# Cross-attention stage of a decoder layer: query and key parts kept in DRAM in blocks of four heads with a gap, each part stored by its own transfer

## The chip, the cores and the metric

One Trainium2 chip, one core of it. The metric is the device time of one execution of the whole kernel in microseconds (us). Before the change it is 2364.4 us, the median of 3 runs (2364.01 to 2364.47).

## The reference, cut to what matters

The kernel computes one decoder layer with the norm behind each part, on 32 sequences of 256 tokens and 256 features: self-attention, cross-attention to 120 context tokens, and a mixture of experts. The change lies in the cross-attention:

```python
q = query @ qw.T + qb            # query: the 256 tokens of a sequence, 16 heads of 16
k = key @ kw.T + kb              # key: its 120 context tokens
v = value @ vw.T + vb
q1, q2 = (q[..., :sd], q[..., sd:])      # each head is cut in two halves of sd = 8
k1, k2 = (k[..., :sd], k[..., sd:])
a1 = softmax(einsum('bhtd,bhsd->bhts', q1, k1) * SCALING)
a2 = softmax(einsum('bhtd,bhsd->bhts', q2, k2) * SCALING)
attn_output = einsum('bhts,bhsd->bhtd', a1 - lam * a2, v)
```

## The kernel before, in words

Four stages run one after the other: `self_attention`, `cross_attention`, `experts`, `finish`. A barrier of all engines stands between the attention stages. The cross stage works through 32 batches, one sequence each, as a software pipeline of steps: in step t a batch t is loaded (X), t-1 is projected (A, lag 1), t-2 has its stacks loaded (B, lag 2), t-3 has the maxima of its scores taken (M, lag 3), t-4 has its scores, exponentials and products with the values computed (S, lag 4), t-5 is put together (O), t-6 is normed and routed to experts (R), and t-7 is scattered into the slot table (Q). Buffers have three slots. Every engine runs its own list of a step in a fixed, hand-written order and waits on semaphores; no planner is at work. The middle of the run is a hardware loop over three steps at a time.

To keep the precision of float32 in bf16 matmuls, the projected queries and keys are split into three bf16 parts. ScalarE makes part 0 (line 1341), GpSimd the rest (1618), ScalarE part 1 (1373), GpSimd part 2 (1623). The tile `parts` has 128 partitions, one for each pair of a dimension d (8) and a head h (16), with d the slower one, and 2 x 256 query and 2 x 120 key columns for each part (the factor 2 is the two halves e of a head). A matmul needs d on the partitions and the heads along the row, so the parts are turned around through DRAM. Lines 1011 to 1015 store them with four transfers for a batch (for each e one for q, one for k, all three parts in one). Lines 984 to 990 load them back: a row of DRAM that holds all 16 heads of one (part, d) becomes one partition of `q_stack` (16 x 256 elements of 2 bytes, 8192 bytes) or `k_stack` (16 x 120, 3840 bytes). `STACK_LOADS` has seven loads for each e (four for q with 8, 8, 16 and 16 rows, three for k with 24, 16 and 8), because parts repeat in the stack: six pairs of parts by 8 dimensions make 48 rows. So 14 loads a batch bring 96 rows of 8192 and 96 rows of 3840 bytes.

All these transfers are issued by SyncE (SP). Its list of a step is: x and context of X (970, 971), residual of S (976), wait for the parts of B in DRAM (980) and for the scores that used its slot (983), the 14 stack loads of B (989), the stores of R and Q (993, 996), wait for the transposed maxima of M and three small loads of them into the last rows of `q_stack` (999 to 1002), wait for part 2 of A (1007), and the stores of the parts of A (1011 to 1015).

TensorE (PE) first uses the stacks of batch B in `max_scores(B, 0)` (line 1053), which waits for all 14 loads (line 1045) and stands behind `scores(S, 5)` in the step. Behind it in the same step comes the transpose of the maxima of M (1218), which ScalarE copies (1381) and SP waits for at line 999 (DMA of line 1001). VectorE reduces each set of max scores (1423). ScalarE's line 1340 waits until the parts of the batch before are in DRAM, before it overwrites them. GpSimd (POOL) scatters batch Q into the slot table with 12 indirect DMAs (1592): seven at the start of its step, three behind line 1618, two behind line 1623.

```python
q_dram = nc.dram_tensor("cross_q_parts", [3, E, NP, P, T], BF16, kind="Internal").ap()
sp.dma_start(q_dram[A.slot][e].rearrange("t p n -> p t n"), parts[:, :, e * T:(e + 1) * T])
q_src = q_dram[B.slot][e].rearrange("t (d h) n -> (t d) (h n)", h=NH)
sp.dma_start(stack[e * HALF + row:e * HALF + row + m, B.slot, 0:NH * n], src[src_row:src_row + m, :])
```

## Time and profile before

| what | us |
|---|---|
| median of 3 runs | 2364.4 |
| the profiled execution, its own time | 2375.9 |
| span of the profile, first to last instruction | 2374.1 |
| busy in the span: PE | 1805.2 (76%) |
| busy: VectorE (DVE) | 1297.7 (55%) |
| busy: GpSimd (POOL) | 1230.5 (52%) |
| busy: ScalarE (ACT) | 1085.8 (46%) |
| q1, the DMA queue of SP: share of the 16 DMA engines' time | 45.8% |

A share of busy time is a mean over four stages with different limits. The cross stage lies between about 807 and 1935 us of the span. "Idle before" of an instruction is the time its engine stood still just before it, and the name behind it is what the profile holds to have ended that: "issue" where it shows nothing, "remote" where the semaphore was raised at a moment at which the profile has no instruction ending. SPq are the DMA issues of SP; their duration is the time of the issue, not of the transfer.

### The profile page before, as it was taken

What the parts mean: (1) busy time and instruction counts of PE and PEld (TensorE: products, weight loads), DVE (VectorE), ACT (ScalarE), POOL (GpSimd) and SP (SyncE); (2) the same over time, 40 slices, a digit from 0 to 9 for tenths busy, and PEclk for the clock granted to TensorE, in tenths of its full rate; (3) what the DMA queues carried; (4) which work ended last, traced back from release to release, by engine and by line L of the source; (5) the groups of instructions that cost most, each with busy time, mean ns of one, the idle gap of its engine ahead of it and who ended that gap; (6) DMA issues with size and microseconds to landing.
All of it is one profiled execution on the core that took longest, in us unless ns stands there. A gap on an engine that the chain in (4) does not pass through costs nothing. (4 is left out here: it accounts for less than half of the span.)

```text
span 2374.1 us, 46091 instructions
## 1 busy us (share of the span) xinstructions
PE 1805.2 (76%) x14688; PEld 1268.9 (53%) x14688; DVE 1297.7 (55%) x3032; ACT 1085.8 (46%) x1670; POOL 1230.5 (52%) x1287
## 2 busy tenths in 40 slices
PE   1499999999998458777778788777887619999900
PEld 1366666666666335545545455454553308888800
DVE  2457667776677247665556655566565412222258
ACT  0356666666666236555555555555553302222200
POOL 1557667766773112555555555555555444554523
PEclk9799999999999769888788777887876759999955
DMA  5656766676665266444444344543342024555545
GB/s 184 138 137 147 175 152 155 157 173 153 158 152 123 69 110 129 87 88 72 89 93 90 75 71 90 93 93 79 73 76 52 17 57 109 131 126 124 113 110 180
DMA packets 288970, 267.14 MB, mean 113 GB/s; under 512 B 78962, under 2 KB 273364, under 8 KB 278640
## 3 DMA queue, kind: packets, MB, share of 16 engines
q1 hardware_dynamic: 257648, 244.57, 45.8%
q0 software_dynamic: 22528, 13.03, 3.7%
q10 hardware_dynamic: 8704, 8.39, 1.1%
q8 instruction: 50, 0.82, 0.2%
q14 instruction: 40, 0.33, 0.1%
HBM read 170.57 MB, written 94.30 MB: 112 GB/s over the span
## 5 line engine op out<-in xcount | busy, mean ns | idle before, releaser
L1423 DVE TENSOR_REDUCE cross_nmax<-cross_p_mx 128x8 f32<-128x960 f32 x256 | 295.2, 1153 | 351.6 <-DMA self_q_stack<-self_nmaxT 220.6
L1592 POOL DMA_INDIRECT slot_table<-cross_tok_i,cross_slot_i x384 | 379.6, 989 | 126.9 <-issue 107.0
L598 DVE TENSOR_REDUCE self_nmax<-self_p_mx 128x2 f32<-128x512 f32 x512 | 329.0, 687 | 209.8 <-PE self_p_mx L340 209.5
L1279 ACT ACTIVATE cross_probs<-cross_p_sc 120x1024 f32<-120x1024 f32 x256 | 261.5, 1021 | 113.4 <-PE cross_p_sc L1037 81.4
L510 ACT ACTIVATE self_probs<-self_p_sc 128x1024 f32<-128x1024 f32 x256 | 261.3, 1021 | 94.7 <-PE self_p_sc L328 92.4
L1069 PE MATMUL cross_p_pv<-cross_probs,cross_v_aug 120*32 120x256 f32 x2048 | 199.2, 462 | 14.4 <-ACT cross_o_raw L1287 5.8
L340 PE MATMUL self_p_mx<-self_k_stack,self_q_stack 96*128 96x256 bf16 x1024 | 160.4, 277 | 64.4 <-DMA self_k_stack<-self_k_parts 60.6
L1053 PE MATMUL cross_p_mx<-cross_k_stack,cross_q_stack 48*128 48x120 bf16 x2048 | 118.5, 247 | 119.2 <-DVE cross_nmax L1423 86.8
L1037 PE MATMUL cross_p_sc<-cross_q_stack,cross_k_stack 51*128 51x256 bf16 x1024 | 118.4, 317 | 85.6 <-issue 47.4
L1053 PEld LDWEIGHTS cross_p_mx<-cross_k_stack,cross_q_stack 48*128 48x128 bf16 x2048 | 83.8, 111 | 162.0 <-DVE cross_nmax L1423 115.0
L328 PE MATMUL self_p_sc<-self_q_stack,self_k_stack 99*128 99x256 bf16 x1024 | 156.8, 276 | 13.6 <-ACT self_probs L510 12.8
L1939 POOL DMA_INDIRECT expert_sums<-ffn_ye,ffn_idx_add x64 | 92.3, 1442 | 121.6 <-DMA expert_sums<-ffn_ye,ffn_idx_add 65.5
L1618 POOL TENSOR_TENSOR cross_qk_rest<-cross_qk,cross_parts 128x752 f32<-128x752 f32 x32 | 51.6, 1613 | 188.5 <-ACT cross_parts L1341 188.5
L340 PEld LDWEIGHTS self_p_mx<-self_k_stack,self_q_stack 96*128 96x128 bf16 x1024 | 95.8, 98 | 92.0 <-DMA self_k_stack<-self_k_parts 46.1
L355 PE MATMUL self_p_pv<-self_probs,self_v_aug 128*32 128x256 f32 x2048 | 140.5, 393 | 1.4 <-ACT self_probs L510 1.4
L1879 DVE COPY ffn_xgT<-ffn_p 128x384 f32<-128x384 f32 x32 | 17.8, 558 | 224.4 <-PE ffn_p L1809 224.4
L699 POOL TENSOR_TENSOR self_even_cos<-self_qkb,self_cos_t 128x512 f32<-128x512 f32 x32 | 40.9, 1280 | 187.6 <-ACT self_qkb L526 187.6
L328 PEld LDWEIGHTS self_p_sc<-self_q_stack,self_k_stack 99*128 99x128 bf16 x1024 | 86.6, 98 | 93.3 <-ACT self_probs L510 49.8
L1857 ACT ACTIVATE ffn_hT<-ffn_ph 128x512 f32<-128x512 f32 x64 | 38.2, 597 | 210.1 <-PE ffn_ph L1827 193.4
L1827 PE MATMUL ffn_ph<-ffn_xT,ffn_sw 128*128 128x256 f32 x512 | 117.7, 383 | 0.0
L1287 ACT ACTIVATE cross_o_raw<-cross_p_pv 128x512 f32<-128x512 f32 x128 | 76.3, 596 | 88.7 <-PE cross_p_pv L1069 49.6
L1800 PE MATMUL ffn_p<-ffn_sw,ffn_hT 128*128 128x256 f32 x512 | 115.9, 379 | 0.0
(180 smaller groups left out, 3852.5 us busy)
## 6 DMA issues: line engine op xcount, KB each, us to landing
self_q_stack<-self_q_parts SPq DMA_DIRECT2D x64, 256.0 KB, 5.8
cross_q_stack<-cross_q_parts SPq DMA_DIRECT2D x128, 128.0 KB
ffn_w<-in_ffn_w SPq DMA_DIRECT2D x64, 256.0 KB
self_q_parts<-self_parts SPq DMA_DIRECT2D x32, 384.0 KB, 2.8
self_k_parts<-self_parts SPq DMA_DIRECT2D x32, 384.0 KB, 3.8
self_k_stack<-self_k_parts SPq DMA_DIRECT2D x32, 384.0 KB, 8.0
cross_q_parts<-cross_parts SPq DMA_DIRECT2D x64, 192.0 KB
expert_sums<-zero_rows SPq DMA_DIRECT2D x8, 1024.0 KB, 10.2
```

Source lines behind the costliest of these rows:

```text
L328: mm = pe.matmul(p_sc[:, w, kc * T:(kc + 1) * T], k_stack[0:RM, S.slot, k_at:k_at + P], q_stack[0:RM, S.slot, u * T:(u + 1) * T], start=Tr ...
L340: mm = pe.matmul(p_mx[:, m % 2, c * T:(c + 1) * T], q_stack[0:RK, M.slot, q_at:q_at + P], k_stack[0:RK, M.slot, m * T:(m + 1) * T], start= ...
L355: mm = pe.matmul(p_pv[j * SLOT:(j + 1) * SLOT, (p % 2) * T:(p % 2 + 1) * T], v_aug[:, S.slot, kc, u, :], probs[:, (u // 2) % 4, (2 * (u % ...
L510: act.activation(probs[:, g % 4, :], p_sc[:, :, :].rearrange("p b n -> p (b n)"), ACT.Exp, scale=SCALE).then_inc(s_exp, 1)
L598: dve.tensor_reduce(nmax[:, M.slot, :, m], p_mx[:, m % 2, :].rearrange("p (c k) -> p c k", c=TC), AX_X, ALU.max, negate=True).then_inc(s_r ...
L1037: mm = pe.matmul(p_sc[:, e, hh * T:(hh + 1) * T], k_stack[r:r + RM, S.slot, h * KEYS:h * KEYS + P], q_stack[r:r + RM, S.slot, h * T:(h + 1 ...
L1053: mm = pe.matmul(p_mx[:, e, (2 * hh + c) * KEYS:(2 * hh + c + 1) * KEYS], q_stack[r:r + RK, M.slot, q_at:q_at + P], k_stack[r:r + RK, M.sl ...
L1069: mm = pe.matmul(p_pv[j * SLOT:(j + 1) * SLOT, (g % 2) * T:(g % 2 + 1) * T], v_aug[0:KEYS, S.slot, e, 2 * g + hh, :], probs[0:KEYS, g % 4, ...
L1279: act.activation(probs[0:KEYS, g % 4, :], p_sc[0:KEYS, :, :].rearrange("p b n -> p (b n)"), ACT.Exp, scale=SCALE).then_inc(s_exp, 1)
L1423: dve.tensor_reduce(nmax[:, M.slot, :, :, 2 * m:2 * m + 2].rearrange("p c e h -> p e h c"), p_mx[:, :, 0:4 * KEYS].rearrange("p e (x k) -> ...
L1592: pool.indirect_dma_start(out=route[:, :], out_offset=bass.IndirectOffsetOnAxis(ap=slot_i[:, Q.slot, tc, k:k + 1], axis=0), in_=tok_i[:, Q ...
L1827: mm = pe.matmul(p_h[:, k // 2, (k % 2) * T:(k % 2 + 1) * T], sw1[:, f, k * P:(k + 1) * P], xT[:, f, :], start=(f == 0), stop=(f == FC - 1))
```

## The change

The DRAM tensors of the parts get another shape. A part is no longer 128 rows of n columns (n = 256 for q, 120 for k), but 32 blocks. A block holds four heads of one dimension, 4 x n elements, and 32 unused elements (64 bytes) behind them. A stack row is then four pieces of 2048 bytes (q) or 960 bytes (k) that don't touch in DRAM, in place of one run of 8192 or 3840 bytes. There are still 14 loads a batch. Each of the three parts is stored by a transfer of its own: 12 stores a batch in place of 4, with the same bytes. The counts that wait for the stores grow by the factor 3 (NP).

```diff
+    PIECE, GAP = 4, 32
-    q_dram = nc.dram_tensor("cross_q_parts", [3, E, NP, P, T], BF16, kind="Internal").ap()
-    k_dram = nc.dram_tensor("cross_k_parts", [3, E, NP, P, KEYS], BF16, kind="Internal").ap()
+    q_dram = nc.dram_tensor("cross_q_parts", [3, E, NP, P // PIECE, PIECE * T + GAP], BF16, kind="Internal").ap()
+    k_dram = nc.dram_tensor("cross_k_parts", [3, E, NP, P // PIECE, PIECE * KEYS + GAP], BF16, kind="Internal").ap()
...
-                    n_pw = held(sp, 64 * (B.turn + 1))
+                    n_pw = held(sp, 64 * NP * (B.turn + 1))
...
-                        q_src = q_dram[B.slot][e].rearrange("t (d h) n -> (t d) (h n)", h=NH)
-                        k_src = k_dram[B.slot][e].rearrange("t (d h) n -> (t d) (h n)", h=NH)
+                        q_src = q_dram[B.slot][e].rearrange("t (d b) x -> (t d) b x", b=NH // PIECE)
+                        k_src = k_dram[B.slot][e].rearrange("t (d b) x -> (t d) b x", b=NH // PIECE)
                         for is_q, row, src_row, m in STACK_LOADS:
                             stack, src, n = (q_stack, q_src, T) if is_q else (k_stack, k_src, KEYS)
-                            sp.dma_start(stack[e * HALF + row:e * HALF + row + m, B.slot, 0:NH * n],
-                                         src[src_row:src_row + m, :]).then_inc(s_st[B.slot], 16)
+                            sp.dma_start(stack[e * HALF + row:e * HALF + row + m, B.slot, 0:NH * n]
+                                         .rearrange("p (b x) -> p b x", x=PIECE * n),
+                                         src[src_row:src_row + m, :, 0:PIECE * n]).then_inc(s_st[B.slot], 16)
...
                     for e in range(E):
-                        sp.dma_start(q_dram[A.slot][e].rearrange("t p n -> p t n"),
-                                     parts[:, :, e * T:(e + 1) * T]).then_inc(s_pw[A.slot], 16)
-                        sp.dma_start(k_dram[A.slot][e].rearrange("t p n -> p t n"),
-                                     parts[:, :, QW + e * KEYS:QW + (e + 1) * KEYS]).then_inc(s_pw[A.slot], 16)
+                        for t in range(NP):
+                            sp.dma_start(q_dram[A.slot][e][t][:, 0:PIECE * T].rearrange("r (i n) -> r i n", n=T),
+                                         parts[:, t, e * T:(e + 1) * T]).then_inc(s_pw[A.slot], 16)
+                            sp.dma_start(k_dram[A.slot][e][t][:, 0:PIECE * KEYS].rearrange("r (i n) -> r i n", n=KEYS),
+                                         parts[:, t, QW + e * KEYS:QW + (e + 1) * KEYS]).then_inc(s_pw[A.slot], 16)
...
-                        act.wait_ge(s_pw[last.slot], 64 * (last.turn + 1))
+                        act.wait_ge(s_pw[last.slot], 64 * NP * (last.turn + 1))
```

## Rows read from the trace of the kernel before

**Rows 1.** Waits, 900 to 1790 us: us in total, times, longest.

```profile
DVE cross_nmax L1423 <- DMA self_q_stack<-self_nmaxT: 201.2, 28, 8.1
...
PEld cross_p_mx L1053 <- DMA cross_k_stack<-cross_k_parts: 3.0, 1, 3.0
```

**Rows 2.** Timeline, one steady step: start us, us, engine, line [idle before].

```profile
1298.99 1.10 POOL L1592 DMA_INDIRECT slot_table<-cross_tok_i,cross_slot_i  x1 [0.84 <-POOL cross_tok_i L1608]
...
1306.80 0.97 POOL L1592 DMA_INDIRECT slot_table<-cross_tok_i,cross_slot_i  x1 [0.30 <-issue]
...
1309.16 1.16 DVE L1423 TENSOR_REDUCE cross_nmax<-cross_p_mx 128x8 f32<-128x960 f32 x1 [7.98 <-DMA self_q_stack<-self_nmaxT]
```

**Rows 3.** Timeline, a step of the drain, behind the last stack loads.

```profile
1837.82 0.97 POOL L1592 DMA_INDIRECT slot_table<-cross_tok_i,cross_slot_i  x1 [0.30 <-issue]
...
1840.95 0.28 ACT L1349 ACTIVATE cross_gate_e<-cross_p_b 128x128 f32<-128x128 f32 x1 [7.61 <-remote]
```

**Rows 4.** Windows: stretch, its length, busy us of PE, PEld, DVE, ACT, POOL, PEclk, DMA share, GB/s.

```profile
1308.00:1310.00 2.00, 0.39 (x4) 0.11 (x4) 0.84 (x1) 1.44 (x3) 0.00 (x0) 0.94 0.01 0
1301.00:1309.00 8.00, 4.01 (x38) 2.59 (x37) 0.18 (x1) 2.23 (x4) 5.25 (x6) 1.00 0.58 109
1825.00:1841.00 16.00, 11.59 (x80) 5.71 (x76) 3.13 (x4) 3.24 (x5) 10.72 (x11) 0.61 0.02 1
```

**Rows 5.** Timeline of SP and PE, the same steady step.

```profile
1300.30 1.14 SPq L989 DMA_DIRECT2D cross_k_stack<-cross_k_parts  x3
...
1319.75 0.49 PE L1053 MATMUL cross_p_mx<-cross_k_stack,cross_q_stack 48*128 48x120 bf16 x8
...
1322.21 1.65 SPq L1001 DMA_DIRECT2D cross_q_stack<-cross_nmaxT  x3
...
1355.55 1.64 SPq L1001 DMA_DIRECT2D cross_q_stack<-cross_nmaxT  x3
```

**Rows 6.** Waits of the DMA queue of SP, 900 to 1790 us.

```profile
SPq L1001 <- ACT cross_nmaxT L1381: 507.2, 28, 20.1
```

**Rows 7.** Waits, 826 to 950 us.

```profile
PE cross_p_mx L1053 <- DMA cross_k_stack<-cross_k_parts: 20.0, 3, 14.9
```

**Rows 8.** Timeline of PE, 826 to 947 us: max scores of a newly loaded batch.

```profile
848.61 0.58 PE L1053 MATMUL cross_p_mx<-cross_k_stack,cross_q_stack 48*128 48x120 bf16 x8 [14.86 <-DMA cross_k_stack<-cross_k_parts]
...
887.65 0.38 PE L1053 MATMUL cross_p_mx<-cross_k_stack,cross_q_stack 48*128 48x120 bf16 x8 [2.38 <-DMA cross_k_stack<-cross_k_parts]
...
931.22 0.38 PE L1053 MATMUL cross_p_mx<-cross_k_stack,cross_q_stack 48*128 48x120 bf16 x8
```

**Rows 9.** Timeline of SP and PE, one whole turn of the early steps.

```profile
889.74 1.60 SPq L1001 DMA_DIRECT2D cross_q_stack<-cross_nmaxT  x3
891.45 0.38 SPq L1012 DMA_DIRECT2D cross_q_parts<-cross_parts  x1
...
892.98 0.52 SPq L1014 DMA_DIRECT2D cross_k_parts<-cross_parts  x1
...
894.65 0.47 SPq L976 DMA_DIRECT2D cross_x_res<-x_with_bias  x1
896.92 1.69 SPq L989 DMA_DIRECT2D cross_q_stack<-cross_q_parts  x4
...
909.00 0.38 PE L1053 MATMUL cross_p_mx<-cross_k_stack,cross_q_stack 48*128 48x120 bf16 x8 [2.72 <-DMA cross_k_stack<-cross_k_parts]
...
911.22 1.60 SPq L1001 DMA_DIRECT2D cross_q_stack<-cross_nmaxT  x3
```

**Rows 10.** Windows behind the loads of 917.7 to 924.6 us, columns as in group 4.

```profile
930.00:931.00 1.00, 1.00 (x9) 0.70 (x8) 0.90 (x4) 0.68 (x3) 0.00 (x0) 1.00 0.15 53
```

**Rows 11.** DMA issues of the whole run: KB each, median us to landing.

```profile
self_q_stack<-self_nmaxT SPq DMA_DIRECT2D x96, 8.0 KB, 1.9
```

**Rows 12.** Windows: 8192-byte rows at the start of the run, then stack loads alone.

```profile
20.00:23.00 3.00, 0.00 (x0) 0.00 (x0) 0.00 (x0) 0.00 (x0) 0.00 (x0) 1.00 1.03 429
852.00:862.00 10.00, 8.16 (x51) 6.22 (x52) 4.94 (x5) 1.21 (x3) 0.00 (x0) 0.50 0.80 99
```

## The prediction

> **What bounds the kernel now.** The change touches only how the parts reach the stacks, so the question is where anything waits for them. I read the waits of the cross stage first. Between 900 and 1790 us, where the pipeline is full, VectorE's reduction stands idle for 201.2 us in 28 waits, 7.2 us each, and the name behind it is a DMA; TensorE waits for the stack loads once, for 3.0 us [rows 1]. The first row is tempting: it falls into the time of the stack loads. The DMA named is one of the self stage, long over, so the name is no evidence. Next I read the timeline of one step. POOL begins seven scatters at 1298.99 and ends them at 1307.77 (1306.80 + 0.97); VectorE's idle time of 7.98 us ends 1.4 us later, at 1309.16 [rows 2]. In the drain, where no stack is loaded any more, the same thing happens behind twelve scatters: the last ends at 1838.79, and ScalarE's idle time of 7.61 us ends at 1840.95, put down to "remote" [rows 3]. The DMA share is 0.58 in the first stretch and 0.02 in the second [rows 4]. So the stall goes with the scatters of GpSimd and not with the stack loads. It sets the steady step of 33.3 us (1322.21 to 1355.55) [rows 5].
>
> The stack loads of that step are issued by 1301.4, the DMA engines are empty from 1308 on (share 0.01), and TensorE first needs them at 1319.75 [rows 4, 5]. That is about 11.7 us of slack. SP itself waits 18.1 us a step (507.2 us in 28 waits) for the transposed maxima [rows 6].
>
> The early steps are different. Before the scatters begin, a turn takes 21.5 us (889.74 to 911.22) [rows 9], and three waits of TensorE, 20.0 us together, are for the stack loads [rows 7]: 14.86 at the first batch, 2.38 at the third, 2.72 at the fourth [rows 8, 9]. There the loop maxima, stores, loads, max scores, maxima is closed through SP's list, and what SP does longer makes the turn longer.
>
> **Eight more stores.** Four stores take 1.53 us for three spacings (891.45 to 892.98), 0.51 us each [rows 9]. Twelve take 8 x 0.51 = 4.1 us more. Queued behind them on SP are x, context, residual and the stack loads. Against that stands the wait for the parts to land. Now the loads start at 896.92, 3.9 us behind the last store's issue, though SP has issued x, context and residual by 895.1 [rows 9]: the four stores (564 KB) are still under way. Spread over 6 us, all but the last are done, and the last holds 30 KB. A transfer of 8 KB lands 1.9 us after its issue [rows 11]; I take 2.4 us. That gives back 1.5 us, and at most 1.8, since the three issues behind the stores still have to be made; at least nothing. So the loads start 4.1 - 1.5 = **2.6 us** later (2.3 to 4.1). The data of the stores is the same, and its runs stay 512 and 240 bytes.
>
> **Pieces of 2048 and 960 bytes.** 14 loads as before, so no more issues; a third dimension may lengthen an issue from 0.4 towards the 0.51 of the stores, at most 14 x 0.1 = 1.4 us, most of it beside the transfers. What the pieces do to the transfers the trace doesn't show; bounds: while stack loads run alone, 12.8 engines are busy (0.80 x 16) and move 99 GB/s, 7.7 GB/s each. Stores of 8192-byte rows from 128 partitions moved 429 GB/s on 16 engines, 26 each [rows 12]. So a row of 8192 bytes is not slow by its length; the engines of a stack load, which has 8 to 24 rows on neighbouring partitions, get in each other's way. The pieces go to the same partitions in the same order. If they cured it, the burst from 896.92 to 909.00, 12.1 us, could shrink to its issue, 14 x 0.4 = 5.6, and one landing, 1.9: 7.5 us, a gain of 4.6 [rows 9, 11]. If the fourfold number of pieces costs, I bound it with 2 us. I take **0.5 us** more, near the old value, since the bytes and partitions stay.
>
> The Trainium skill (SBUF — State Buffer, section "Door 1: The DMA port swizzle") says that the bandwidth of a DMA goes by how many of 16 ports its partitions reach; by it the burst would not change, and the gain of 4.6 falls away. Against the change speaks DMA: Bandwidth & Descriptors, section "How a descriptor splits into AXI transactions": a piece that starts off a 256-byte boundary costs an extra transaction. Blocks of 2112 bytes mostly start off one; my estimate from its beats is up to 12% of the burst, 1.4 us a turn, or 5 us in the sum.
>
> **What of it reaches the end.** A turn that is bound by the loads grows by 2.6 + 0.5 = 3.1 us.
> - First, third and fourth batch: 3 x 3.1 = 9.3.
> - Second batch: no wait in the view now [rows 7]; its loads queue behind the first batch's and move with them. 0 to 3.1, I take 0.4.
> - Fifth batch: TensorE starts on it at 931.22 without a wait, and by 930 to 931 the DMA share is down to 0.15 [rows 8, 10]. Some 1.2 us of cover, so 3.1 - 1.2 = 1.9.
> - The other 27: slack 11.7 against 3.1, cover left. Nothing. If that cover were gone, each turn would pay the excess.
> - Gap and counts: nothing. ScalarE's wait for the stores (line 1340) stands in the next step, behind three exponentials; the turn of 21.5 us or more covers stores that end 4.1 us later.
>
> Sum: 9.3 + 0.4 + 1.9 = 11.6 us. A turn lost early isn't won back, because the later steps are bound by something else and just start later. The profiled execution took 2375.9 us for its span of 2374.1; the median without a profile is 2364.4, 0.5% less. I add the 11.6 to the median: **2376.0 us**. About 0.2%, 4.7 us, is what a measurement of this kernel can tell from no change.
>
> **Rivals.**
> - *A, the pieces free the DMA engines.* For it: 7.7 GB/s an engine against 26 [rows 12]. Against: same partitions, same order. A bound turn then changes by 2.6 - 4.6 = -2.0; three turns -6, the fifth batch nothing: 2358.4. Chance 0.15.
> - *B, long rows make the stall.* If scatters stood behind 8192-byte rows and pieces let them pass, the 7.2 us of 27 steps would go: 2364.4 - 194 + 12 = 2182. Against it stands the drain, with the stall and no loads [rows 3, 4]. Chance 0.04.
> - *C, much slower.* The end of the steady stall is set by whichever ends last, scatters or loads burst. The burst ends near 1308, the scatters at 1307.8 [rows 2, 4]: 3.1 us more would make the burst the last, from any growth over about 0.5 us on. Then 27 steps pay some 2.6 more: 2376 + 70 = 2446. Against it again the drain. Chance 0.08.
> - *D, no change.* The pieces save in the transfer what the stores cost in issue (burst 2.6 us shorter): 2364.4, give or take 4.7. Chance 0.20. That the change would not do what it says (pieces merged back to rows) is hardly possible with the gap between them; it would come out near the forecast, by the stores alone.
>
> **How the numbers follow.** The forecast has 0.53: between 7 us (only the third and fourth batch pay, and the least) and 28 us (4.1 + 2 in 4.5 turns). For 8 in 10 the range takes in A and D below and ends above at 28 us: 2358 to 2392; B, C and the edges stay outside. Faster by over 0.2%: A and B, 0.19. Within 0.2%: D and a small part of the forecast's low edge, 0.22. Slower by over 0.2%: 0.59.
>
> **What the changed profile would show.** SP's stores: 12 a batch, spaced near 0.5 us. The early turn: 24 to 25 us in place of 21.5, with TensorE's waits for the stacks near 18, 5 and 6 us. The steady turn: still 33 us, VectorE's wait still about 7.2 us, SP's wait for the maxima down from 18.1 to about 15. Windows with loads alone: if GB/s per busy engine is well above 7.7, A or D holds. A steady turn other than 33.3 would prove me wrong about what binds it, up for C and down for B. The packet count must grow by 32 x 192 x 3 = 18432.

## The result: 2.5% slower, outside the range

The changed kernel takes 2422.4 us (median of 4 runs, 2412.8 to 2429.1) against 2364.2 for the kernel before beside it (4 runs, 2362.1 to 2364.5): a ratio of 1.025, 95% interval 1.022 to 1.028. The forecast was 2376.0 with a range up to 2392. The sign was right, the size was a fifth of what came: +11.6 forecast, +58 measured.

The profiled execution took 2422.3 us for its span of 2420.5, 46.4 more than the span of before. (The profiled execution of before was 12 us above its median, which is why the spans differ by less than the medians.)

### The profile after

The page's line on the DMA packets:

```profile
DMA packets 311499, 267.16 MB, mean 110 GB/s; under 512 B 83058, under 2 KB 289748, under 8 KB 304240
```

Before there were 288970. The difference is 22529: the forecast 18432 for the pieces, 8 x 32 x 16 = 4096 for the eight additional stores of a batch (the kernel with the stores alone, e1_stores, has 4097 more than before), and one. So the change does what it says.

The waits after, from 826 to 950 us and from 900 to 1790 us, and those of SP's queue from 900 to 1790 (us in total, times, longest). They answer to [rows 7], [rows 1] and [rows 6]:

```profile
PE cross_p_mx L1056 <- DMA cross_k_stack<-cross_k_parts: 34.5, 4, 18.9
...
DVE cross_nmax L1426 <- DMA self_q_stack<-self_nmaxT: 206.9, 25, 8.9
...
SPq L1003 <- ACT cross_nmaxT L1384: 254.1, 26, 11.2
```

TensorE's waits for the stack loads in the early stretch grew from 20.0 to 34.5 us. VectorE's wait behind the scatters is longer, 8.3 us each against 7.2. SP has 9.8 us left in a step, where it had 18.1.

One early turn after, timeline of SP and PE, as [rows 9]:

```profile
898.29 1.70 SPq L1003 DMA_DIRECT2D cross_q_stack<-cross_nmaxT  x3
900.11 0.57 SPq L1015 DMA_DIRECT2D cross_q_parts<-cross_parts  x1
900.73 0.60 SPq L1017 DMA_DIRECT2D cross_k_parts<-cross_parts  x1
...
907.46 0.60 SPq L1017 DMA_DIRECT2D cross_k_parts<-cross_parts  x1
...
909.46 0.46 SPq L977 DMA_DIRECT2D cross_x_res<-x_with_bias  x1
910.03 2.76 SPq L990 DMA_DIRECT2D cross_q_stack<-cross_q_parts  x4
912.84 2.64 SPq L990 DMA_DIRECT2D cross_k_stack<-cross_k_parts  x3
915.51 2.62 SPq L990 DMA_DIRECT2D cross_q_stack<-cross_q_parts  x4
918.17 2.11 SPq L990 DMA_DIRECT2D cross_k_stack<-cross_k_parts  x3
...
923.39 0.58 PE L1056 MATMUL cross_p_mx<-cross_k_stack,cross_q_stack 48*128 48x120 bf16 x8 [8.45 <-DMA cross_k_stack<-cross_k_parts]
...
926.68 1.71 SPq L1003 DMA_DIRECT2D cross_q_stack<-cross_nmaxT  x3
```

Cut at the same four points, the turn of before [rows 9] and this one are:

| piece of the turn, us | before | after | more | forecast |
|---|---|---|---|---|
| maxima issued to first store | 1.71 | 1.82 | 0.1 | 0 |
| first store to first stack load | 5.47 | 9.92 | 4.5 | 2.6 |
| first stack load to max scores | 12.08 | 13.36 | 1.3 | 0.5 |
| max scores to the next maxima | 2.22 | 3.29 | 1.1 | 0 |
| turn | 21.48 | 28.39 | 6.9 | 3.1 |

Four q loads now take 2.6 to 2.8 us to issue, 0.66 to 0.69 each, where they took 1.69 or less.

With stack loads alone on the queue (860 to 870 us, the columns of [rows 4]) the busy engines move 81 / (0.64 x 16) = 7.9 GB/s each, where it was 7.7 [rows 12]:

```profile
860.00:870.00 10.00, 6.86 (x47) 4.53 (x45) 4.32 (x7) 3.74 (x8) 2.21 (x2) 0.67 0.64 81
```

One steady step after, timeline of SP, POOL and DVE, as [rows 2] and [rows 5]:

```profile
1330.76 1.10 POOL L1595 DMA_INDIRECT slot_table<-cross_tok_i,cross_slot_i  x1 [0.84 <-POOL cross_tok_i L1611]
1333.09 2.79 SPq L990 DMA_DIRECT2D cross_q_stack<-cross_q_parts  x4
...
1338.56 0.97 POOL L1595 DMA_INDIRECT slot_table<-cross_tok_i,cross_slot_i  x1 [0.30 <-issue]
...
1340.78 2.12 SPq L990 DMA_DIRECT2D cross_k_stack<-cross_k_parts  x3
1341.43 1.16 DVE L1426 TENSOR_REDUCE cross_nmax<-cross_p_mx 128x8 f32<-128x960 f32 x1 [8.48 <-DMA self_q_stack<-self_nmaxT]
```

The seven scatters still take 8.8 us. The loads, which before were all issued by 2.5 us into the scatters [rows 2, 5], now go out from 2.3 us into them until 3.4 us past their end. The stall ends while loads are still being issued, so it isn't the loads' end that ends it.

**Where the 46 us are.** I cut the cross stage at the first exponential of each batch (line 1279, after: 1282), a start that each timeline has. From the first store to the first of them: 42.7 us before, 47.7 after, +5.0. The three steps behind it: 22.6 and 29.1 each, +19.4. The next three: 31.0 and 33.1, +6.4. The 24 of batches 6 to 30: 32.78 and 33.50, +17.3. Together +48, and the self stage happened to end 2.1 earlier. So some 31 us lie in the start, where 11.6 were forecast, and 17 in the steady steps, where none were. The mean steady step before is 32.8 us; the 33.3 of the prediction was one step. A second profile of each kernel (below) has 32.4 and 33.4, so steady steps of one kernel differ by up to 0.4 us between profiles.

### The profile page after: what moved, and what is told of

Its sections match the earlier page's. It is cut to its first block and busy times, and to the rows that moved or that the text cites. A ratio compares the mean times of both kernels' runs of the same rounds, so it can differ in the third digit from the quotient of the medians.

```text
span 2420.5 us, 46347 instructions
## 1 busy us (share of the span) xinstructions
PE 1825.1 (75%) x14688; PEld 1284.9 (53%) x14688; DVE 1297.7 (54%) x3032; ACT 1083.4 (45%) x1670; POOL 1229.5 (51%) x1287
## 5 line engine op out<-in xcount | busy, mean ns | idle before, releaser
L1072 PE MATMUL cross_p_pv<-cross_probs,cross_v_aug 120*32 120x256 f32 x2048 | 205.0, 475 | 13.8 <-issue 10.4
L1040 PEld LDWEIGHTS cross_p_sc<-cross_q_stack,cross_k_stack 51*128 51x128 bf16 x1024 | 30.9, 99 | 173.4 <-ACT cross_probs L1282 97.6
```

Of the source, the lines that this page charges most:

```text
L1040: mm = pe.matmul(p_sc[:, e, hh * T:(hh + 1) * T], k_stack[r:r + RM, S.slot, h * KEYS:h * KEYS + P], q_stack[r:r + RM, S.slot, h * T:(h + 1 ...
L1072: mm = pe.matmul(p_pv[j * SLOT:(j + 1) * SLOT, (g % 2) * T:(g % 2 + 1) * T], v_aug[0:KEYS, S.slot, e, 2 * g + hh, :], probs[0:KEYS, g % 4, ...
```

## The experiments

Two theories stood at the start. **Theory 1:** SP's longer issues (12 stores, 14 slower loads) are the cost, paid in every turn that is closed through SP, and hidden where VectorE is stalled behind the scatters. **Its rivals:** the steady excess comes from the loads colliding with the scatters, or from the pieces in the transfers.

In the tables below "start" is the mean of the three steps behind the first exponential, "steady" the mean of the 24 from batch 6 to 30, both cut as above, and "issue" the median time from the first to the end of the last store or load of a batch.

One thing has to be known first. The kernel before took 2364 to 2367 us beside the runs of some experiments and 2204 to 2205 us beside others, always the same within a group of runs that shared a chip. The slower time was met on two chips, on one of them twice, the faster on three others. What differs is the stall behind the scatters, which is there at 2364 us and missing at 2205. I call them chips with and without the stall; whether it is the chip, or something else that stayed the same for a group of runs, isn't shown. Ratios are always to the kernel before on the same chip.

### Stores alone, loads held, and no scatters (a chip without the stall)

e1_stores: twelve dense stores, whole rows loaded (the counts grow by NP as in the change).

```diff
-sp.dma_start(q_dram[A.slot][e].rearrange("t p n -> p t n"), parts[:, :, e * T:(e + 1) * T])
+for t in range(NP):
+    sp.dma_start(q_dram[A.slot][e][t], parts[:, t, e * T:(e + 1) * T])   # k alike
```

> The dense layout and whole-row loads of before, with twelve stores a batch in place of four. Theory SP (the change costs what SyncE issues longer; early turns pay it in full, because stores and loads close the loop there, and steady steps pay a part because the load issues slide under the scatters and deepen their stall): stores take 4 to 6 us more of SP, the load issues stay at 5.3 us; early turns 24 to 26 us instead of 21.5, steady step up by 0.2 to 0.5 us; in all 20 to 33 us slower than before, about half of the change's 58. Rival pieces (the small pieces are what costs, in the transfers): at most 12 us slower. If it gave the full 58, the pieces would cost nothing.

e3_before_noscat and e4_after_noscat: the kernel before, and the changed one, without the scatters into the slot table and the waits for them, so the experts work on a table that isn't filled. Only their cross stages are read.

```diff
 def scatter(Q, at):
-    for x in at:
+    for x in []:
```

> Before, with the scatter of token numbers into the slot table left out (so the experts stage works on empty slots; only the cross stage is to be compared). If the stall of some 8 us a step is made by back-to-back scatters, the steady step falls from 33.3 us to between 22 and 26 us, near the 21.5 to 24 us of the early turns, VectorE's wait of 7.2 us is gone, and the total falls by 180 to 280 us. Rival (the stack loads make the stall): the step stays above 31 us and the idle time stays.

> The changed kernel, with the same scatter left out. Theory SP: without the stall the loop of maxima, stores, loads and max scores binds every step, so each step pays what the early turns of the changed kernel pay, 27 to 30 us a step against 22 to 26 without the change: 4 to 7 us a step, 120 to 200 us slower than the same kernel without the change. Rival (only scatters and small pieces together cost): no more than 20 us slower than it.

e5_hold: the kernel before, stack loads held until ScalarE has copied x2T.

```diff
 n_pw = held(sp, 64 * (B.turn + 1))
+n_r2 = held(sp, R.n + 1) if R.on else None
 sp.wait_ge(s_wts, 16)
+if R.on:
+    sp.wait_ge(s_r2, n_r2)
```

> Before, with SyncE made to hold the 14 stack loads until the transposed rows of the routed batch are copied (line 1317), some 6 us later in a steady step; nothing is added, no piece is smaller. Theory SP: the load issues now lie wholly under the scatters, as in the changed kernel, and the stall gets longer: steady step up by 0.5 to 1 us (13 to 26 us in all), and 5 to 10 us more where the first held batches are waited for. Rival pieces: the steady step stays at 32.5 us on average, only the 5 to 10 us of the first held batches show.

| kernel, before 2205.0 us | us | ratio | start | steady | issue of stores, loads |
|---|---|---|---|---|---|
| e1_stores | 2214.3 | 1.005 | 25.1 | 26.9 | 5.6, 5.3 |
| e3_before_noscat | 2150.9 | 0.974 | 22.9 | 26.5 | 2.1, 5.3 |
| e4_after_noscat | 2238.1 | 1.016 | 29.6 | 28.9 | 7.7, 9.8 |
| e5_hold | 2276.8 | 1.032 | 23.5 | 29.6 | 2.1, 5.3 |

Without scatters the change costs 87 us, and the steady step grows by 2.4 us. In these steps nothing stalls, and the loop of the start goes on to the end. The hold, which makes SP's loads late and nothing longer, costs 72 us here: without the stall the loads have less slack than the hold takes. The expectations had reckoned with a chip that has the stall. The removal of the scatters brought only 54 us in place of 180 to 280, since there was no stall to remove; the change cost 87 in place of 120 to 200 without them; and the twelve stores cost 9 us where 20 to 33 were expected.

### One part of the change at a time (a chip with the stall)

The kernel before and the changed one again, then two kernels with about half of the change each. e7_piece16 has the stores and the gap but whole rows; e2_pieces16 has the four stores of before and 16 pieces a row. Neither is an exact half: the stores of e7_piece16 write 8 blocks and not 32, and its packet count (289995) is 1025 above that of before, where 12 dense stores (293068) are 4098 above, so its stores are split otherwise.

```diff
-PIECE, GAP = 4, 32          # e7_piece16, from the changed kernel
+PIECE, GAP = 16, 32
```

```diff
-"cross_q_parts", [3, E, NP, P, T]          # e2_pieces16, from the kernel before
+"cross_q_parts", [3, E, NP, P, T + 32]     # k alike; stores write 0:T
-q_src = q_dram[B.slot][e].rearrange("t (d h) n -> (t d) (h n)", h=NH)
+q_src = q_dram[B.slot][e].rearrange("t (d b) x -> (t d) b x", b=NH)
```

> The kernel before, unchanged, profiled a second time. The first profile of it had VectorE idle for 7.2 us in 27 steps behind the slot-table scatters of GpSimd, and 2374 us of span; the runs of the kernel before beside the last experiments took about 2205 us. Theory 1 (the stall behind the scatters is not always there): where it takes about 2205 us the idle time of 7.2 us a step has gone, the steady step is 27 us, and TensorE's waits for the stack loads are found in most steps. Theory 2 (the 160 us are the clock's): the granted clock is far above 0.85 and the stall is still there, 5 us or more a step.

> The changed kernel, unchanged, beside the kernel before. Theory 1 (issues on SP's queue are what the change costs, +3.6 to 5.7 us of store issue and +4.5 of load issue a turn, and the stall behind the scatters covers most of it where it is there): if the kernel before takes about 2205 us here, without the stall, every turn pays what was paid only in the early turns, 2 to 3 us, and the changed kernel takes 2205 + 32 x 2.5 = 2285, ratio 1.03 to 1.045. If the kernel before takes 2364 us, 2422 again, ratio 1.025. Theory 2 (the change costs a fixed 50 to 60 us wherever it runs, by early turns and collisions): ratio 1.025 in either case.

> The changed kernel with the block made 16 heads long: twelve stores and a gap behind each stack row, but a stack row comes in one piece again. Theory 1 (the pieces make the load's issue long: 0.69 us in place of 0.38 each, 14 a batch): an issue is back at 0.38 us, the 14 at 5.3 us, and of the excess over the kernel before only the stores' part is left, 9 to 15 us of the time, as with the twelve stores alone. Theory 2 (it is the gap, that is rows that start off a boundary, that costs, and not the number of pieces): the loads' burst is as long as with four pieces and the excess stays above two thirds of the change's.

> The kernel before with four stores, but a gap of 64 bytes behind every part row, so that a stack row loads in 16 pieces of 512 or 240 bytes. Theory 1 (the issue of a load grows with its number of pieces): 14 x (0.38 + 0.31 x 15/3) = 27 us of issue a batch, past what any step has to spare: at least 10 us more a step, ratio above 1.1. Theory 2 (the issue grows once, by the third dimension, whatever the number of pieces): 9.8 us as with four pieces, and the time 1 to 2 % above the kernel before, below the changed kernel, since it has only four stores. Theory 3 (the number of pieces costs in the transfer): issue as theory 2, but the burst from first issue to TensorE's start 3 us or more longer than its issue.

Then the dense stores and the hold once more, on this kind of chip:

> Twelve stores of one part each, no gap, stack rows loaded whole: the kernel that was 1.0047 times the time of before at 2205 us. The changed kernel with one piece a row, that is this one with a gap, was 1.0122 times before at 2365 us. Theory 1 (the stores' longer issue is the whole of it, the gap nothing): at 2365 us 1.010 to 1.014, the steady step within 0.3 us of the one with the gap. Theory 2 (the gap costs): 1.006 or less, and a spacing of the stores of 0.5 us in place of 0.64.

> The kernel before with the stack loads of a steady step held on SP until the copy of the projected x, some 6 to 8 us later than now; nothing else on SP's queue gets longer. It was 1.032 times before at 2205 us, where no stall is. Theory 1 (with the stall of 8 us a step the loads have 11.7 us of slack, so lateness alone costs nothing in a steady step): where the kernel before takes 2364 us the steady step stays within 0.3 us of 32.4 and TensorE has no waits for the stacks. Theory 2 (lateness of SP's list is what costs 1 us a step in the changed kernel, slack or not): the step grows by 1 us or more, 2390 to 2400 us or above.

| kernel, before 2364.7 (last two 2363.8) us | us | ratio (95%) | start | steady | issue of stores, loads |
|---|---|---|---|---|---|
| c_before, one run | 2361.2 | | 21.4 | 32.4 | 2.0, 5.3 |
| c_after | 2423.7 | 1.0253 (1.0224 to 1.0282) | 30.3 | 33.4 | 7.7, 9.8 |
| e7_piece16: 12 stores, gap, whole rows | 2395.1 | 1.0122 (1.0092 to 1.0152) | 28.0 | 32.7 | 7.4, 5.3 |
| e8_stores_again: 12 dense stores | 2384.1 | 1.0101 (1.0068 to 1.0134) | 25.3 | 32.9 | 5.6, 5.3 |
| e2_pieces16: 4 stores, 16 pieces | 2404.4 | 1.0174 (1.0142 to 1.0206) | 26.9 | 33.1 | 2.0, 9.8 |
| e9_hold_again | 2351.4 | 0.9960 (0.9936 to 0.9984) | 24.1 | 31.6 | 2.0, 5.3 |

The timeline of SP in the two halves of the change, first e2_pieces16, then e7_piece16:

```profile
1252.35 2.72 SPq L989 DMA_DIRECT2D cross_q_stack<-cross_q_parts  x4
1255.12 2.14 SPq L989 DMA_DIRECT2D cross_k_stack<-cross_k_parts  x3
```

```profile
1282.24 0.57 SPq L1015 DMA_DIRECT2D cross_q_parts<-cross_parts  x1
1282.86 0.57 SPq L1017 DMA_DIRECT2D cross_k_parts<-cross_parts  x1
```

And e8_stores_again, dense:

```profile
1266.64 0.43 SPq L1013 DMA_DIRECT2D cross_q_parts<-cross_parts  x1
1267.12 0.43 SPq L1015 DMA_DIRECT2D cross_k_parts<-cross_parts  x1
```

- **The issue of a load grows in one jump.** A load of whole rows takes 5.3 / 14 = 0.38 us to issue, with 4 pieces 9.8 / 14 = 0.70, with 16 pieces 0.70 as well. It is the third dimension of the access that costs, not how many pieces there are; the time of e2_pieces16, +40 us with the four stores of before, is theory 2 of its expectation and excludes theory 1.
- **The stores' issue depends on their access, too.** A dense store of one part is spaced 0.475 us, one into blocks 0.61 (e7) or 0.64 (the change). In the change that is 2.1 of the 5.6 us by which the stores' issue grew. The start shows it: 28.0 in e7 against 25.3. In the third to fifth batch 1.7 us of that lie between the first store and the first load, and 0.5 between the max scores and the next maxima. The expectation for e7, 9 to 15 us for the stores, missed: they cost 30, with dense stores 20. A load of whole rows with a gap behind each is not slower to issue or to land (5.3 us; from the first load to the max scores 884.39 to 895.51 and 910.01 to 922.90, 11.1 and 12.9 us, against 10.7 and 12.4 in c_before), so behind whole rows the gap costs at most the 0.5 us a turn of these differences.
- **The number of pieces shows in the landing.** From the first load to the max scores, mean of the third to fifth batch, c_before takes 11.8 us, c_after 14.2 and e2_pieces16 16.6 (two of its three: 902.55 to 918.40, 928.10 to 944.89). In the last two kernels 9.8 of it are issue, so 16 pieces cost 2.4 us more than four at the same issue. That is theory 3 of that expectation beside theory 2, though its sign (3 us beyond the issue) doesn't tell them apart: whole rows, too, take 6.0 us beyond their issue.
- **The halves overlap.** 30 us for the stores and 40 for the pieces are 70; both together cost 59. In the steady steps the halves (32.7, 32.9 and 33.1 us) are hardly beyond the 0.4 us by which two profiles of one kernel differ; the 33.4 of the whole change is.
- **Late loads alone cost nothing while the stall is there.** The hold was 3.2% slower without the stall and is 0.4% faster with it. Its steady step is 0.8 us shorter than before, which neither theory had.

### The stall broken up

e6_spread and e10_after_spread: the twelve scatters of a batch in four groups of three in place of seven, three and two; in the kernel before and in the changed one.

```diff
-scatter(Q, range(0, 7))
+scatter(Q, range(0, 3))
...
-scatter(Q, range(7, 10))
+scatter(Q, range(3, 6))
...
-scatter(Q, range(10, 12))
+scatter(Q, range(6, 9))
...
 pool.tensor_tensor(shift[:, :], neg_mean[:, :], rstd[:, :], ALU.mult)
+if Q.on:
+    scatter(Q, range(9, 12))
```

> The kernel before, with the slot-table scatters of a batch in four groups of three (three places in GpSimd's list of the step that were used with seven, three and two of them, and a fourth behind the shift) in place of seven, three and two. Theory 1 (the 7 to 8 us stall of every steady step needs the seven scatters in a row; three in a row leave none): VectorE's idle time over 4 us goes in all 24 steps, the steady step falls from 32.4 towards the 26.5 us of the kernel without scatters, the time to about 2364 - 24 x 5 = 2240 where the kernel before takes 2364, and nothing changes where it takes 2205. Theory 2 (twelve scatters cost what they cost, wherever they stand): the step stays at 32 us, with four idle times of 2 us in place of one of 8.

> The changed kernel with the same four groups of three scatters. Theory 1 (the stall is time in which SP's longer list is hidden; without it the steady turn is closed through SP's stores and loads): the changed kernel gains less from the spreading than the kernel before does, its steady step is near 28.9 us against 26.5, TensorE waits for the stack loads in most steps, and the excess over the kernel with the four groups alone is 80 to 90 us, as it was without any scatters (2238 against 2151). Theory 2 (the change's cost in the steady steps comes from its DMA issues under the scatters): the excess is smaller than the 59 us that it is with the stall, 30 to 40 us, the early turns alone.

Both ran where the kernel before takes 2363.8 us. e6_spread: **2214.3 us, ratio 0.939 (0.935 to 0.943)**, steady step 26.8. e10_after_spread: 2342.6 us, 0.993 (0.990 to 0.995), steady step 30.5. Their waits from 980 to 1740 us, first those of e6_spread, then of e10_after_spread:

```profile
DVE cross_nmax L1423 <- DMA self_q_stack<-self_nmaxT: 32.8, 27, 6.8
```

```profile
PE cross_p_mx L1056 <- DMA cross_k_stack<-cross_k_parts: 116.7, 25, 6.4
...
DVE cross_nmax L1426 <- DMA self_q_stack<-self_nmaxT: 28.0, 12, 4.0
```

VectorE's idle time behind the scatters falls from 179.2 us in this stretch (below) to 32.8, and the step by 5.6 us. In the changed kernel the stall goes as well, but TensorE now waits for the stack loads in every step, 4.7 us each. The change costs 128 us between these two, more than twice the 58 with the stall: the stall was hiding it. Expected were 80 to 90, so the closed loop is right in kind; its size is more than I had.

### The changed kernel where the stall is missing

> The changed kernel, unchanged. Where the kernel before takes 2364 us: ratio 1.025 again. Where it takes 2205 us, theory 1 (the stall hides SP's longer list; without it each turn of 27 us is closed through SP): TensorE waits for the stacks in most steady steps, step 29 to 30 us in place of 27, 2290 us or more, ratio 1.035 to 1.05. Theory 2 (a fixed cost of 50 to 60 us wherever it runs): ratio 1.025.

> The changed kernel, with the stack loads of a steady step held until the copy of the projected x. In the kernel before the same hold made the steady step 0.8 us shorter (31.6 in place of 32.4). Theory 1 (the steady excess of 1.0 us, 33.4 against 32.4, comes from DMA issues while the scatters run, which let fewer of TensorE's completions through; lateness costs nothing): the step falls to 32.5 or less, the time to 2400 or below. Theory 2 (the excess is lateness of SP's list, since in the changed kernel the loads end only 3 to 4 us before TensorE wants them): the hold takes the last cover, TensorE waits for the stacks in the steady steps and the step grows by 2 us or more, 2470 or above.

> The changed kernel with the stack loads of a steady step held until the copy of the projected x. At 2205 us it was 1.061 times the kernel before. Theory 1 (in the steady steps with the stall it is issues under the scatters that cost, not lateness): where the kernel before takes 2364 us, 2400 or below, the step 32.5 or less. Theory 2 (the changed kernel's loads have no cover left): step 34.5 or more, TensorE waits for the stacks, 2450 or above.

All three ran on chips without the stall. The changed kernel took 2321.7 us beside 2204.2: **ratio 1.055 (1.052 to 1.059)**, +117 us; start 30.1, steady 30.2. Its waits from 980 to 1740 us:

```profile
PE cross_p_mx L1056 <- DMA cross_k_stack<-cross_k_parts: 136.4, 25, 7.8
```

The same change costs 2.5% on one chip and 5.5% on another. Theory 2, a fixed cost, is out. The scatters have a share here as well: with them the change costs 117 us, without any 87, and from the first load to the max scores a steady turn takes 14.9 us in e15_after_again and 13.8 in e4_after_noscat. So the rival that loads and scatters collide holds for about 1 us a turn on these chips. With the loads held too (the edit of e5_hold in the changed kernel) it is 1.061 in both runs (2341.0 beside 2205.2, 2338.9 beside 2204.2), steady 31.1. Neither run of the hold fell on a chip with the stall. An estimate of the cover there comes from the traces: where TensorE waits for them, loads need 14.9 us from the first issue to the max scores (e15_after_again, mean of the steady batches), whole rows 13.7 (e5_hold). With the stall the steady steps of c_after leave them 18.0, those of c_before 22.5. So some 3 us of cover are left of 9.

### What costs in a steady step with the stall

There the hold says that lateness isn't it, and yet the changed kernel pays 0.7 to 1.0 us a step. The last experiment adds twelve small writes of a constant behind each batch's stack loads, to DRAM rows that nothing reads. Each moves 4 KB, so an issue and its small transfer come together. The end of the stage alone waits for them.

```diff
+for j in range(12):
+    sp.dma_start(idle_dram[B.n][j], ident[0:8, :]).then_inc(s_idle, 16)
```

> The kernel before, with twelve more DMA issues on SP right behind the stack loads of each batch: each writes 8 rows of 512 bytes of a constant to a DRAM row that nothing reads, and nothing waits for them but the end of the stage. The stack loads are issued no later than before; SP's list is some 5 us longer, while it has 18 us to spare in a steady step. Theory 1 (issues under the scatters are what costs in a steady step): the idle time of VectorE grows by 0.3 us or more and the steady step by 0.5 to 1.0 us, 2376 to 2388 in all. Theory 2 (only late stores and loads cost): the steady step stays at 32.4 within 0.2, the time within 5 us of the kernel before, since the stores, too, wait for ScalarE in the steady steps.

> The kernel before with twelve more issues behind each batch's stack loads. At 2205 us, where the stall behind the scatters is missing, they cost nothing (ratio 0.9993). Theory 1 (issues while the scatters hold back TensorE's completions lengthen that stall): where the kernel before takes 2364 us, VectorE's idle time grows by 0.3 us or more and the steady step by 0.5 to 1.0 us, ratio 1.005 to 1.010. Theory 2 (only late stores and loads cost): ratio 0.998 to 1.002 there as well.

> The kernel before with twelve more issues behind each batch's stack loads, for a case in which the kernel before takes 2364 us (at 2205 us they cost nothing, ratio 1.000). Theory 1 (issues while the scatters hold back TensorE's completions lengthen the stall): steady step 0.5 to 1.0 us longer than 32.4, ratio 1.005 to 1.010. Theory 2 (only late stores and loads cost): ratio 0.998 to 1.002.

Without the stall they cost nothing: 2203.1 beside 2205.2 (0.9993, 0.998 to 1.001) and 2201.2 beside 2204.2 (1.000, 0.998 to 1.002). With it: **2391.6 beside 2366.8, ratio 1.0115 (1.0077 to 1.0154)**, steady step 33.7, while the start of 22.5 us stays in the spread of the kernel before (21.4 and 22.6 in two profiles). In these steps SP still waits 12 us for the maxima (272.0 us in 760), and no wait of the four engines in this stretch names a stack load, or one of the two stores behind the idle writes. The timeline of SP, first in the run with the stall, then in e14_idle_again:

```profile
1300.68 1.13 SPq L991 DMA_DIRECT2D cross_k_stack<-cross_k_parts  x3
1301.99 8.82 SPq L994 DMA_DIRECT2D idle_rows<-cross_ident  x12
1311.53 0.39 SPq L997 DMA_DIRECT2D x_and_gates<-cross_y_sb  x1
```

```profile
1319.10 5.48 SPq L994 DMA_DIRECT2D idle_rows<-cross_ident  x12
```

The same twelve issues take 8.8 us under the scatters on the one chip and 5.5 on the other. The stack loads show no such difference: 9.8 us for the 14 of the changed kernel under the scatters of either kind of chip. The waits from 980 to 1740 us show where the time goes; c_before, c_after, e16_idle_third and e9_hold_again in this order:

```profile
DVE cross_nmax L1423 <- DMA self_q_stack<-self_nmaxT: 179.2, 27, 8.0
...
ACT cross_o_raw L1287 <- remote: 33.4, 24, 4.0
ACT cross_qk L1325 <- remote: 32.0, 17, 2.9
ACT cross_x2T L1317 <- remote: 29.4, 10, 3.6
ACT cross_probs L1279 <- remote: 22.7, 19, 2.3
```

```profile
DVE cross_nmax L1426 <- DMA self_q_stack<-self_nmaxT: 186.4, 24, 8.7
...
ACT cross_qk L1328 <- remote: 58.8, 20, 4.4
...
ACT cross_x2T L1320 <- remote: 41.5, 11, 6.1
ACT cross_probs L1282 <- remote: 29.7, 20, 2.5
ACT cross_o_raw L1290 <- remote: 12.5, 8, 3.0
```

```profile
DVE cross_nmax L1428 <- DMA self_q_stack<-self_nmaxT: 175.7, 22, 8.2
ACT cross_qk L1330 <- remote: 85.8, 21, 5.2
...
ACT cross_x2T L1322 <- remote: 54.2, 13, 5.7
ACT cross_probs L1284 <- remote: 10.5, 7, 2.9
```

```profile
DVE cross_nmax L1426 <- DMA self_q_stack<-self_nmaxT: 133.5, 22, 7.9
...
ACT cross_o_raw L1290 <- remote: 88.1, 24, 4.8
...
ACT cross_probs L1282 <- remote: 6.7, 7, 1.6
```

"Remote" is a semaphore raised at a moment at which the profile has no instruction ending. Added up (with the small rows left out above) ScalarE's are 117.5 us in the kernel before, 147.0 in the changed one, 155.2 with the idle writes and 99.9 with the hold. With VectorE's and over the steps in 760 us (760 / 32.4 = 23.5, 22.8, 22.6, 24.1) that is 12.6, 14.6, 14.6 and 9.7 us a step, and the steps are 32.4, 33.4, 33.7 and 31.6. (The waits of two engines overlap, so such a sum is a sign and not a time.) Without the stall these ScalarE rows are missing altogether, in the kernel with idle writes and in the changed one.

So the longer steady steps go with longer waits of VectorE and ScalarE around the scatters, and twelve small writes that nothing waits for are enough to make a step longer: by 1.3 us, a little more than expected. VectorE's wait, which theory 1 had grow by 0.3 us or more, hardly does (175.7 / 22.6 = 7.8 us a step against 7.6); ScalarE's do. That the change's eight stores and slower loads cost their 1.0 us in the same way is likely by this and not shown. How an issue does it no row shows, and it isn't the mere number under the scatters: the hold puts nearly all 14 loads there (they begin 3.9 us after the first of the seven; in the kernel before the loads begin 3 us ahead of it) and is the fastest of the four. Whether it matters when in the scatters the issues fall, or whether it is the transfer and not the issue, stays open.

## Why the prediction was wrong, point by point

- **What bounds the steady step** was right: the stall goes with the scatters, not with the stack loads. e6_spread moves only scatters and takes 5.6 us out of each step. Rival B, that long rows make the stall, fell: with pieces the wait is 8.3 us. Rival C, that it ends with the later of scatters and burst, fell too: it ended at 1341.43, while loads were still being issued until 1342.9. Its number for the step, 33.3 us, was one step's; the mean was 32.8, so a steady step of 33.5 is a change and not the standstill that it looks like beside 33.3.
- **Eight more stores: right parts, one of them mis-sized.** The spacing was taken as 0.51 us from the stores of before [rows 9]; a store into blocks is spaced 0.64. From the first to the end of the last store there are now 7.95 us against 2.05, +5.9 where the sum had 4.1. The 1.5 us given back for the landing were right: 5.9 - 1.5 = 4.4, and that piece grew by 4.45.
- **The pieces: the failed bound.** "At most 14 x 0.1 = 1.4 us, most of it beside the transfers": measured are 14 x 0.32 = 4.5 us. The issue was bounded by the nearest row, the 0.51 of a store, and a row of another access isn't a bound. It also isn't wholly beside the transfers: from the first load to the max scores the early turn above grew by 1.3 us, and the mean of the third to fifth batch by 0.75 us in that pair (12.87 to 13.62, with some slack in the fifth of before) and by 2.4 in the later pair on one chip (11.8 to 14.2). The forecast was 0.5, its upper bound 2.
- **Rivals A and D** (pieces free the DMA engines, or save what the stores cost) fell: with the burst longer and not shorter there is nothing of the 4.6 us, and the 7.9 GB/s of a busy engine isn't well above 7.7, which was their sign. The Trainium skill (SBUF — State Buffer, section "Door 1: The DMA port swizzle") had the bandwidth go by the partitions reached; the trace agrees so far that pieces to the same partitions gained nothing. It isn't the whole, though: 16 pieces a row, to the same partitions and with the same issue, took 2.4 us longer than four. My estimate from the Trainium skill (DMA: Bandwidth & Descriptors, section "How a descriptor splits into AXI transactions") had up to 12% of the burst, 1.4 us a turn, for pieces that start off a boundary. Redone with the page's beats it is smaller, still an estimate: 268 beats in place of 256 for a q row, nothing for a k row, whose blocks are 1024 bytes apart, so 3% or 0.4 us. No run separates such a share; whole rows with a gap have one such start each and test it hardly.
- **What reaches the end: too few turns, and a term that was left out.** Four and a half turns were to pay. All five early batches wait for their stacks, 18.9, 1.9, 5.3, 8.5 and 5.7 us, against the forecast of 18, 5 and 6 for three; the second and the fifth were not covered. Each turn also lost 1.1 us between the max scores and the next maxima, where nothing had been put down. There TensorE ran its first eight max scores in 0.58 us against 0.38 [rows 9]. It had stood still for 8.45 us, and its granted clock from 923.3 to 926.7 us was 0.50, the lower of its two levels; before, behind 2.72 us, it was 0.85 on the mean of 909 to 911. The start costs 31 us, not 11.6.
- **"The other 27: nothing" failed, though its slack was real.** The hold shows the slack: 0.4% faster with loads that are issued 11.8 us behind the first store in place of 5.0. The sum put down nothing because nobody waits for the loads there, and in the changed kernel nobody does either; yet 24 steps pay 0.7 to 1.0 us, 17 to 24 us. "Cover" was read from the waits for the loads alone. The idle writes show that small DMAs which nobody waits for can cost 1.3 us a step beside this stall; by which way the change's issues do it stays open.
- **The sentence "If that cover were gone, each turn would pay the excess"** held: without the stall the change costs 117 us (a chip that hasn't got it) to 128 (scatters spread), and TensorE waits for the stacks in nearly every step.
- **SP's wait** was forecast at 15 us a step and is 9.8: 18.1 minus the 3.1 of the sum, where it should have lost the additional issue, up to 5.6 + 4.5; it lost 8.3.
- **The range** held the bounds of terms that were themselves too narrow. With the issue of a load bounded by its double, a turn could have grown by 2.6 + 5.3 = 7.9 us and five turns by 40, and the range would have reached 2404. The steady steps' part lay outside every term but rival C's. The lower edge of 7 us doesn't follow from its terms either: two turns at the least 2.3 + 0.5 are 5.6.

## What to carry to other kernels

Count a DMA's issue apart from its transfer, and measure the issue for the very access that it will have: one more dimension took a load from 0.38 to 0.70 us, with 4 pieces and with 16 alike. A loop that closes through one issuing queue pays each such microsecond once a turn; a stall elsewhere hides it only so long as the stall stands, so look at the stall first: here a few lines that spread the scatters are worth 150 us on a chip with the stall, more than the change ever cost (without the stall they weren't run). And measure on more than one chip where a stall has no cause that the profile names.

## What the runs showed of the hardware that I had not expected

- Behind seven indirect DMAs in a row on GpSimd, 1.28 us apart, what waits for TensorE stands still for about 8 us on some chips; behind three in a row it hardly does (VectorE's row is 32.8 us in 760 in place of 179.2). On other chips nothing of it shows (e14_idle_again has no such row): the kernel before takes 2205 us against 2364, a difference of 7% of the whole kernel, while the self stage takes the same on all (the first store of the cross stage is issued at 825.8 to 833.5 us on all of them).
- Twelve small writes issued by SP under the scatters took 0.74 us each on a chip with the stall and 0.46 on one without. The 14 stack loads of the changed kernel took 0.70 each on both.
- With the stall TensorE's granted clock is lower as well. In two kernels from 980 to 1740 us, c_before and e14_idle_again (stretch, its length, busy us of PE, PEld, DVE, ACT, POOL, PEclk, DMA share, GB/s):

```profile
980.00:1740.00 760.00, 608.33 (x5492) 387.90 (x5492) 472.23 (x1158) 409.39 (x662) 410.24 (x513) 0.80 0.44 85
```

```profile
980.00:1740.00 760.00, 626.14 (x6250) 396.44 (x6250) 564.40 (x1387) 454.87 (x743) 491.03 (x628) 0.86 0.50 95
```

The first shows 5492 matmuls at a granted clock of 0.80, the second 6250 at 0.86, and e6_spread has 0.90 in the same stretch. How much of its 150 us is the clock's stays open.
